# Scores against the context itself: 64-dimension keys replaced by queries widened to 128 dimensions

## The chip, the cores and the metric

The kernel runs on one core of one Trainium2 chip. The metric is the device time in microseconds of one execution, and the number compared is the median of several. A core has five engines that this kernel uses: TensorE (PE, the matrix engine; PEld is its weight load), VectorE (DVE), ScalarE (ACT), GpSimd (POOL), and SyncE (SP), which starts DMAs. They run side by side and meet at semaphores.

## What is computed

Two layers of gated cross-attention, each with a feed-forward block behind it, over 8 batches of 112 queries (width 512) and 375 context rows (width 128). The attention has 16 heads. Of the reference only this matters here (layer 0; layer 1 is the same without the rotation of `q_big`):

```python
q_hk = (hidden_q @ Wq.T).reshape(Bv, Sv, H, K)
q_big = jnp.einsum('bshk,hkq->bshq', q_hk, w_kc_q)
q_big = _apply_rope(q_big, sin_q[None, :, None, :], cos_q[None, :, None, :])
kv_r = _apply_rope(kv_c, sin_k[None], cos_k[None])
q_r = jnp.einsum('bshq,hqr->bhsr', q_big, W_qr)       # 64 dimensions a head
k_r = jnp.einsum('bld,hdr->bhlr', kv_r, W_kr)         # 64 dimensions a head
scores = jnp.einsum('bhsr,bhlr->bhsl', q_r, k_r)
attn = jax.nn.softmax(scores, axis=-1)
ctx_c = jnp.einsum('bhsl,bld->bhsd', attn, kv_r)
```

`scores` is a product of three matrices, q_r times W_kr transposed times kv_r transposed. It can be multiplied from the right first (keys, then scores over 64 rows) or from the left first (queries widened from 64 to 128 dimensions, then scores over 128 rows with the context). Products of this kind are made in float16 with each operand split in a high and a low part, so each takes three matrix products: high by high, high by low, low by high.

## The kernel before

**Stages.** A start (norms, rotation and transposition of the context into `kvT`), attention of layer 0, its output projection mixed with the middle and the first feed-forward block, attention of layer 1, its output projection, the second feed-forward block. In the profile attention 0 lies at about 40 to 420 us and attention 1 at about 560 to 835 us.

**A pair and its slots.** Attention goes over 8 pairs of heads; a pair has 8 slots, one for each batch. Four tables of lists (TENSOR, SCALAR, VECTOR, GPSIMD, lines 70 to 142), one for each engine and layer, say what the engine does in each slot and in which order. All engines execute in order, so a table is the schedule. The items:

- X, scores of this slot's batch (line 759 on PE): six products of 64x128 weights over 375 columns, heads in the upper and the lower 64 rows of the array in turns. On DVE X is the maximum (line 1114). E is the exponential on ACT (line 982), N the reciprocal on DVE (line 1119) and the normalisation on POOL (line 1279).
- T, transposition of the probabilities of two slots before (line 785), split by ACT (line 992) and DVE (line 1182). There is one PSUM area for scores and one for T, so X waits for the exponentials of the slot before, and T for DVE's split of the slot before.
- S, the weighted sum of three slots before (line 800), copied out by ACT (line 998) and DVE (line 1124).
- K, the keys of one batch (line 771): the weights are W_kr of the pair, the moving side is `kvT`. ACT copies them out (line 1008) and POOL splits them into high and low (lines 1268 and 1271).
- A and B (line 813), layer 0: `q_hk` in four half-pairs of 12 products, and `q_big` in 12 blocks of 3 products. DVE takes a B with two products by the rotation tables (line 1137). SP swaps halves of one block by DMA, POOL adds (line 1260).
- C (line 867), layer 0: q_r of a half of the batches. M, W, F with Q, layer 1: the weights are folded first, and F and Q (line 813) make q_r of a half.
- G (line 873) turns W_qr, R (line 877) turns W_kr; U (line 882) prepares the output weights. L and H are the splits of the loaded weights (lines 1193 and 1040), V is work for the feed-forward weights.

**Banks.** Everything but X and T goes round the four PSUM banks 2 to 5 in the order of the PE table. So each group waits until the group four places before it has been taken out by ACT, DVE or both:

```python
bank_of = {g: 2 + i % 4 for i, g in enumerate(groups)}
```

**Last pair.** When there is no next pair to prepare, PE fills the slots with heads of the output projection (line 524; HEADS_AHEAD, lines 147 to 152, says how many).

## Time and profile before

| | us |
|---|---|
| Median of 3 runs | 1024.25 (1022.31 to 1024.72) |
| The profiled execution | 1024.81 |
| Its span, first to last instruction | 1022.8 |
| PE busy / DVE / ACT / POOL | 953.1 / 664.3 / 529.2 / 520.5 |
| Mean granted TensorE clock | 0.987 of full speed |

PE is the busiest engine at 93% of the span; the others are busy for half to two thirds of it. The page gives sums for the whole span, and the stages differ, so the rows below are read from single pairs and slots. A matrix product's bar in the timeline is longer than the time it keeps the array (bars overlap), so what a group costs PE is the distance from its start to the next group's start.

### The profile page before, as it was taken

The page shows a single profiled execution, that of the slowest core. Times are in us where ns is not written, and L with a number is a line of the kernel's source. Part 1 is how long each engine was busy: PE and PEld are TensorE (multiplying, and loading weights), DVE is VectorE, ACT ScalarE, POOL GpSimd, SP SyncE. Part 2 cuts the span into 40 slices and gives each one's busy share as a digit, 9 for nine tenths or more (in the row PEclk, how much of TensorE's full clock was granted, in tenths as well). Part 3 has the DMA queues.
Part 4 walks back from the last instruction along what each step waited for, and adds up shares of the span by engine and source line. Part 5 has one row for each costly group of instructions (what it writes and reads, how often), then busy time and mean ns, then how long its engine had stood idle before and what let it go on. Part 6 is the DMA issues. An engine that isn't in the chain of part 4 may idle for free. (4 is left out here: it accounts for less than half of the span.)

```text
span 1022.8 us, 19581 instructions
## 1 busy us (share of the span) xinstructions
PE 953.1 (93%) x6132; PEld 566.9 (55%) x6141; DVE 664.3 (65%) x1180; ACT 529.2 (52%) x1238; POOL 520.5 (51%) x652
## 2 busy tenths in 40 slices
PE   3679999999999999999889899999999999989998
PEld 1335555555555655644344567777777764445443
DVE  4789777787878787488677757666666653413012
ACT  2255666665766665600377367777777762116300
POOL 4477777776868777405224266665666651200000
PEclk9799999999999999999999999999999999999999
DMA  8214233232314132063020111222012006004001
GB/s 255 66 39 117 61 95 85 69 107 55 115 51 121 49 105 81 15 207 121 0 84 21 61 63 63 72 72 72 14 57 72 1 1 230 7 19 157 1 31 41
DMA packets 30344, 75.56 MB, mean 74 GB/s; under 512 B 4967, under 2 KB 11239, under 8 KB 28126
## 3 DMA queue, kind: packets, MB, share of 16 engines
q1 hardware_dynamic: 24706, 66.31, 20.5%
q10 hardware_dynamic: 5596, 8.70, 3.1%
q8 instruction: 25, 0.41, 0.2%
q14 instruction: 17, 0.14, 0.0%
HBM read 63.98 MB, written 3.68 MB: 66 GB/s over the span
## 5 line engine op out<-in xcount | busy, mean ns | idle before, releaser
L1279 POOL TENSOR_SCALAR scratch<-scratch,rinv 112x375 f32<-112x375 f32 x256 | 154.9, 618 | 138.8 <-DVE rinv L1119 138.8
L982 ACT ACTIVATE scratch<-ps,mxn 112x375 f32<-112x375 f32 x256 | 144.2, 571 | 36.6 <-DVE mxn L1114 35.1
L524 PE MATMUL ps<-arena 128*128 128x512 f16 x672 | 149.3, 379 | 1.2 <-PEq L685 1.2
L1114 DVE TENSOR_REDUCE mxn<-ps 112x2 f32<-112x750 f32 x128 | 119.7, 935 | 41.8 <-PE ps L759 41.3
L1260 POOL TENSOR_TENSOR scratch<-scratch 128x448 f32<-128x448 f32 x64 | 110.7, 1739 | 43.1 <-DVE scratch L1137 27.1
L813 PE MATMUL ps<-xnT,scratch 128*128 128x448 f16 x576 | 124.5, 364 | 6.5 <-DVE scratch L1137 3.3
L800 PE MATMUL ps<-scratch,kvn_hi 125*128 125x224 f16 x768 | 119.9, 260 | 3.3 <-DVE scratch L1159 2.3
L1271 POOL TENSOR_TENSOR scratch<-scratch 128x375 f16<-128x375 f32 x128 | 115.6, 903 | 10.9
L785 PEld LDWEIGHTS ps<-ident,scratch 112*125 112x125 f32 x768 | 101.1, 188 | 26.9 <-issue 19.9
L1182 DVE TENSOR_TENSOR scratch<-ps,scratch 125x672 f16<-125x672 f32 x128 | 108.7, 849 | 5.4 <-ACT scratch L992 5.4
L1137 DVE TENSOR_TENSOR scratch<-ps,ropeq 128x448 f32<-128x448 f32 x192 | 110.0, 616 | 2.1 <-PE ps L813 1.7
L524 PEld LDWEIGHTS ps<-arena 128*128 128x128 f16 x672 | 65.5, 98 | 76.4 <-issue 2.2
L785 PE MATMUL ps<-ident,scratch 112*125 112x112 f32 x768 | 104.8, 272 | 1.1 <-DVE scratch L1182 1.0
L992 ACT ACTIVATE scratch<-ps 125x672 f16<-125x672 f32 x128 | 94.2, 736 | 16.1 <-PE ps L785 15.3
L800 PE MATMUL ps<-scratch,kvn_lo 125*128 125x224 f16 x384 | 99.4, 259 | 0.0
L1159 DVE SCALAR_TENSOR_TENSOR scratch<-ps,scratch 128x448 f16<-128x448 f32 (+2 forms) x88 | 50.0, 569 | 71.8 <-ACT scratch L1026 70.0
L998 ACT ACTIVATE arena<-ps 128x224 f32 (+1 forms) x128 | 45.7, 357 | 95.4 <-PE ps L800 94.7
L1026 ACT ACTIVATE scratch<-ps 128x448 f16<-128x448 f32 (+2 forms) x88 | 43.5, 505 | 89.4 <-PE ps L813 50.5
L813 PEld LDWEIGHTS ps<-xnT,scratch 128*128 128x128 f16 x576 | 57.0, 100 | 59.0 <-issue 9.3
L759 PE MATMUL ps<-scratch 64*128 64x375 f16 x768 | 83.3, 322 | 5.8 <-DVE scratch L1159 4.1
L800 PEld LDWEIGHTS ps<-scratch,kvn_hi 125*128 125x128 f16 x768 | 68.1, 98 | 36.8 <-issue 24.4
L771 PE MATMUL ps<-kvT,scratch 128*128 128x375 f16 x384 | 83.1, 325 | 0.7 <-DVE scratch L1159 0.7
(166 smaller groups left out, 1413.3 us busy)
## 6 DMA issues: line engine op xcount, KB each, us to landing
scratch<-in_wq SPq DMA_DIRECT2D x16, 512.0 KB, 4.5
scratch<-in_wo SPq DMA_DIRECT2D x16, 512.0 KB, 3.7
wabs<-in_w ACTq DMA_DIRECT2D x32, 256.0 KB, 3.0
scratch<-in_w SPq DMA_DIRECT2D x8, 1024.0 KB, 4.9
scratch<-in_W SPq DMA_DIRECT2D x8, 1024.0 KB, 5.9
scratch<-scratch SPq DMA_DIRECT2D x64, 112.0 KB, 2.3
scratch<-in_kcq SPq DMA_DIRECT2D x8, 512.0 KB, 3.4
scratch<-in_qr SPq DMA_DIRECT2D x32, 128.0 KB, 3.3
```

Of the source, the lines that this page charges most:

```text
L524: last = nc.tensor.matmul(ps[:, bank, :], a[:, h, t * P:(t + 1) * P], c[:, h, :], start=(h == 0 and i == 0), stop=(h == H - 1 and i == 2))
L785: last = nc.tensor.transpose(turn_ps[0:LP, c, hh * S:(hh + 1) * S], prob[0:S, s % 2, hh, c * LP:(c + 1) * LP], ident[0:S, 0:S])
L800: last = nc.tensor.matmul(bank(it, ("S", slot))[:, 0:2 * S], kv[0:LP, s, c, :], pr[0:LP, s % 2, cols], start=(c == 0 and i == 0), stop=(c ...
L813: last = nc.tensor.matmul(out, lhs[i](c), rhs[j](c), start=(n == 0), stop=(n == 3 * chunks - 1))
L982: last = nc.scalar.activation(prob[0:S, s % 2, hh, :], scores_ps[0:S, hh, 0:L], ACT.Exp, bias=mxn[0:S, s % 2, hh:hh + 1], accum_out=rsum[0 ...
L992: nc.scalar.activation(probT_hi[0:LP, s % 2, :].rearrange("p (c n) -> p c n", c=LC), turn_ps[0:LP, :, 0:2 * S], ACT.Copy).then_inc(turn_hi ...
L1114: nc.vector.tensor_reduce(mxn[0:S, s % 2, :], scores_ps[0:S, :, 0:L], AX_X, ALU.max, negate=True).then_inc(max_done, 1)
L1137: last = nc.vector.tensor_tensor(dst.rearrange("p (b n) -> p b n", b=B // 2), src, ropeq[:, t:t + 1, :].to_broadcast([P, B // 2, S]), ALU. ...
L1182: nc.vector.tensor_tensor(probT_lo[0:LP, s % 2, :].rearrange("p (c n) -> p c n", c=LC), turn_ps[0:LP, :, 0:2 * S], probT_hi[0:LP, s % 2, : ...
L1260: nc.gpsimd.tensor_tensor(roped[:, u % 2, rows], roped[:, u % 2, rows], turned[:, rows], ALU.add)\
L1271: nc.gpsimd.tensor_tensor(kr_lo[:, b % 2, 0:L], kr[:, b % 2, 0:L], kr_hi[:, b % 2, 0:L], ALU.subtract).then_inc(k_ready, 1)
L1279: last = nc.gpsimd.tensor_scalar(prob[0:S, s % 2, hh, :], prob[0:S, s % 2, hh, :], rinv[0:S, s % 2, hh:hh + 1], P_SCALE, ALU.mult, ALU.mult)
```

## The change

Keys, their copy on ACT and their split on POOL are gone (K), and so is R. Instead the half's 64-row queries (C in layer 0, Q in layer 1) are split into `q64_hi` and `q64_lo`, and a new group P, two banks wide, multiplies them by W_kr: six products of 64x128 weights over 448 columns, heads in the upper and the lower 64 rows of the array in turns. ACT and DVE split each bank of it into `qw_hi` and `qw_lo`, 128 dimensions wide. W_kr is no longer turned by PE; it is split where it was loaded (a third weight split, H 2 on ACT and L 2 on DVE). Scores are six products of 128x128 weights over 375 columns, whose moving side is `kvT`. The weights of a batch differ from product to product.

```diff
-        kr, a = view(scratch, a, [2, LPAD], F32)
-        kr_hi, a = view(scratch, a, [2, LPAD], F16)
-        kr_lo, a = view(scratch, a, [2, LPAD], F16)
-        qr_hi, a = view(scratch, a, [B, P], F16)
-        qr_lo, a = view(scratch, a, [B, P], F16)
+        q64_hi, a = view(scratch, a, [HALF], F16)
+        q64_lo, a = view(scratch, a, [HALF], F16)
+        qw_hi, a = view(scratch, a, [2 * B, P], F16)
+        qw_lo, a = view(scratch, a, [2 * B, P], F16)
...
-                        for i, (a, b) in enumerate(((qr_hi, kr_hi), (qr_hi, kr_lo), (qr_lo, kr_hi))):
-                            for hh in range(2):
-                                rows = slice(hh * R, (hh + 1) * R)
-                                last = nc.tensor.matmul(scores_ps[:, hh, 0:L], a[rows, s, :],
-                                                        b[rows, s % 2, 0:L],
+                        for hh in range(2):
+                            for i, (a, j) in enumerate(((qw_hi, 0), (qw_hi, 1), (qw_lo, 0))):
+                                last = nc.tensor.matmul(scores_ps[:, hh, 0:L], a[:, hh, s, :],
+                                                        kvT[:, j, s * L:(s + 1) * L],
                                                         start=(i == 0), stop=(i == 2))
...
-                        for i, (v, j) in enumerate(((wkr_hi, 0), (wkr_hi, 1), (wkr_lo, 0))):
-                            last = nc.tensor.matmul(bank(p, g)[:, 0:L], v,
-                                                    kvT[:, j, b * L:(b + 1) * L],
-                                                    start=(i == 0), stop=(i == 2))
-                        last.then_inc(k_done, 1)
...
+                            pe.wait_ge(split_lo, nth_half(q, "qr"))
+                            for i, (a, b) in enumerate(((wkr_hi, q64_hi), (wkr_hi, q64_lo),
+                                                        (wkr_lo, q64_hi))):
+                                for h in range(2):
+                                    rows = slice(h * R, (h + 1) * R)
+                                    last = nc.tensor.matmul(bank(p, ("P", n, h))[:, 0:HALF], a[rows],
+                                                            b[rows], start=(i == 0), stop=(i == 2))
...
-                        nc.gpsimd.tensor_copy(kr_hi[:, b % 2, 0:L], kr[:, b % 2, 0:L])\
-                            .then_inc(k_high, 1)
-                        pool.wait_ge(k_high, nth(q, B, b))
-                        nc.gpsimd.tensor_tensor(kr_lo[:, b % 2, 0:L], kr[:, b % 2, 0:L],
-                                                kr_hi[:, b % 2, 0:L],
-                                                ALU.subtract).then_inc(k_ready, 1)
```

The tables are written anew. In layer 0 each preparation group of a next pair comes one slot earlier against X, and the P groups stand in slots 3 and 7, in front of B. In layer 1 they stand in slots 1 and 6. One row of PE's table and one of DVE's, layer 0:

```diff
-    [TURN, SCORES, *ropes(0, 2, 0), ("S", 4), ("K", 6), ("A", 1)],
+    [TURN, SCORES, *wide(1), *ropes(0, 2, 0), ("S", 3), ("A", 1)],
...
-    [SCORES, *ropes(0, 2), TURN, *ropes(0, 0), NORM, ("S", 4), ("A", 1)],
+    [SCORES, TURN, *wide(1), *ropes(0, 2, 0), NORM, ("S", 3), ("A", 1)],
```

**What moves on PE, slot with two B and an A.** Layer 0, the loop over pairs, from the scores on; before, slot 0:

```order
L759 MATMUL ps<-scratch 128x375 x6
L851 REGISTER_ALU
L852 ISA
L813 MATMUL ps<-scratch 128x448 x3
L658 REGISTER_ALU
L813 MATMUL ps<-scratch 128x448 x3
L656 REGISTER_ALU
L800 MATMUL ps<-scratch,kvn_hi 128x224 x2
```

In the changed kernel, slot 3 (L764 is the scores, L862 is P, L806 is B, L793 is S, L670 prepares a wait for a bank):

```order
L764 MATMUL ps<-kvT,scratch 128x375 x6
L833 REGISTER_ALU
L857 REGISTER_ALU
L862 MATMUL ps<-scratch 128x448 x6
L670 ISA
L866 REGISTER_ALU
L806 MATMUL ps<-scratch 128x448 x6
L670 REGISTER_ALU
L793 MATMUL ps<-scratch,kvn_hi 128x224 x2
```

P has come between the scores and the two B. P takes two banks, so S is now the fourth bank after P's first, and waits for DVE to take that one out.

**What moves on DVE, the same slots.** Before (L1114 maximum, L1137 rotation of a B, L1182 split of T), slot 4, whose items are those of slot 0:

```order
L1114 TENSOR_REDUCE mxn<-ps 112x2
L1163 ISA
L1176 REGISTER_ALU
L1137 TENSOR_TENSOR scratch<-ps,ropeq 128x448 x2
L1182 TENSOR_TENSOR scratch<-ps,scratch 125x672
L1163 REGISTER_ALU
L1137 TENSOR_TENSOR scratch<-ps,ropeq 128x448 x2
```

In the changed kernel, slot 3, behind the maximum (L1184 split of T, L1160 of 128x4x112 the low part of a P bank, L1140 rotation):

```order
L1184 TENSOR_TENSOR scratch<-ps,scratch 125x672
L1152 REGISTER_ALU
L1160 SCALAR_TENSOR_TENSOR scratch<-ps,scratch 128x4x112
L1152 REGISTER_ALU
L1160 SCALAR_TENSOR_TENSOR scratch<-ps,scratch 128x4x112
L1164 ISA
L1178 REGISTER_ALU
L1140 TENSOR_TENSOR scratch<-ps,ropeq 128x448 x2
L1164 REGISTER_ALU
L1140 TENSOR_TENSOR scratch<-ps,ropeq 128x448 x2
```

The two low parts of P stand behind the maximum and T's split, and ahead of both rotations.

**What moves on PE where a slot with two B ends.** Before, the end of slot 2 and the start of slot 3 of layer 0 (L771 the keys, L882 U, L785 T):

```order
L800 MATMUL ps<-scratch,kvn_lo 128x224
L662 REGISTER_ALU
L771 MATMUL ps<-kvT,scratch 128x375 x3
L662 REGISTER_ALU
L880 ISA
L882 MATMUL ps<-scratch 128x512
L785 MATMUL ps<-ident,scratch 125x112 x6
L759 MATMUL ps<-scratch 128x375 x6
```

In the changed kernel, the end of slot 1 and the start of slot 2 (L892 is U, L778 is T):

```order
L793 MATMUL ps<-scratch,kvn_lo 128x224
L670 REGISTER_ALU
L890 ISA
L892 MATMUL ps<-scratch 128x512
L778 MATMUL ps<-ident,scratch 125x112 x6
L761 REGISTER_ALU
L764 MATMUL ps<-kvT,scratch 128x375 x6
```

The keys have gone from between S and U, so T follows its slot's S by U alone.

## Rows read from the trace of the kernel before

**Rows 1.** Busy time by engine, one pair of each layer (us, times).

```profile
core 0: us, PE busy (x) PEld busy (x) DVE busy (x) ACT busy (x) POOL busy (x), PEclk, DMA share, GB/s
213.00:259.50 46.50, 45.42 (x311) 27.38 (x309) 37.34 (x69) 29.79 (x76) 34.39 (x41) 1.00 0.30 85
689.80:721.70 31.90, 31.55 (x254) 23.28 (x253) 21.60 (x41) 22.94 (x63) 20.10 (x33) 1.00 0.18 58
```

**Rows 2.** Timeline of PE, layer 0: start us, us, operation; around G and R.

```profile
281.09 0.49 PE L873 MATMUL ps<-ident,scratch 128*128 128x128 f32 x3
282.14 0.33 PE L877 MATMUL ps<-ident,scratch 128*128 128x128 f32 x1 [0.56 <-DVE scratch L1137]
282.50 0.74 PE L813 MATMUL ps<-scratch 128*128 128x448 f16 x3
...
327.59 0.49 PE L873 MATMUL ps<-ident,scratch 128*128 128x128 f32 x3
```

**Rows 3.** Timeline of PE, layer 1, a slot from T to G.

```profile
655.50 0.60 PE L785 MATMUL ps<-ident,scratch 112*125 112x112 f32 x4
656.03 0.65 PE L759 MATMUL ps<-scratch 64*128 64x375 f16 x6
656.62 0.36 PE L800 MATMUL ps<-scratch,kvn_hi 125*128 125x224 f16 x2
...
657.49 0.65 PE L771 MATMUL ps<-kvT,scratch 128*128 128x375 f16 x3
657.97 0.49 PE L873 MATMUL ps<-ident,scratch 128*128 128x128 f32 x3
```

**Rows 4.** Timeline of PE, layer 0: T before slot 0, then slot 2.

```profile
248.70 0.81 PE L785 MATMUL ps<-ident,scratch 112*125 112x112 f32 x6
249.77 0.49 PE L759 MATMUL ps<-scratch 64*128 64x375 f16 x4 [0.26 <-DVE scratch L1159]
...
258.93 0.81 PE L785 MATMUL ps<-ident,scratch 112*125 112x112 f32 x6
259.67 0.65 PE L759 MATMUL ps<-scratch 64*128 64x375 f16 x6
260.25 1.31 PE L813 MATMUL ps<-scratch 128*128 128x448 f16 x6
261.39 0.36 PE L800 MATMUL ps<-scratch,kvn_hi 125*128 125x224 f16 x2
...
262.26 0.64 PE L771 MATMUL ps<-kvT,scratch 128*128 128x375 f16 x3
263.04 1.10 PE L882 MATMUL ps<-scratch 128*128 128x512 f32 x2
263.97 0.81 PE L785 MATMUL ps<-ident,scratch 112*125 112x112 f32 x6
```

**Rows 5.** Timeline of DVE in the same slot 2.

```profile
260.71 0.93 DVE L1114 TENSOR_REDUCE mxn<-ps 112x2 f32<-112x750 f32 x1
261.64 1.16 DVE L1137 TENSOR_TENSOR scratch<-ps,ropeq 128x448 f32<-128x448 f32 x2
262.72 0.85 DVE L1182 TENSOR_TENSOR scratch<-ps,scratch 125x672 f16<-125x672 f32 x1
```

**Rows 6.** Timeline of all engines, last pair of layer 1, one slot of the scores' loop.

```profile
825.56 0.65 PE L759 MATMUL ps<-scratch 64*128 64x375 f16 x6
...
826.26 0.94 DVE L1114 TENSOR_REDUCE mxn<-ps 112x2 f32<-112x750 f32 x1 [0.73 <-PE ps L759]
...
827.11 0.85 DVE L1182 TENSOR_TENSOR scratch<-ps,scratch 125x672 f16<-125x672 f32 x1
827.22 0.36 ACT L998 ACTIVATE arena<-ps 128x224 f16<-128x224 f32 x1 [0.82 <-PE ps L800]
...
828.48 0.21 ACT L982 ACTIVATION_READ_ACCUMULATOR scratch<-ps,mxn 112x1 f32 x1
...
828.92 0.49 PE L759 MATMUL ps<-scratch 64*128 64x375 f16 x4
```

**Rows 7.** Groups by line and shape: ACT's high part and DVE's low part.

```profile
L1159 DVE SCALAR_TENSOR_TENSOR scratch<-ps,scratch 128x448 f16<-128x448 f32 x64 | 39.9, 624 | 60.9 <-ACT scratch L1026 59.0
L1026 ACT ACTIVATE scratch<-ps 128x448 f16<-128x448 f32 x64 | 35.1, 548 | 77.5 <-PE ps L813 50.5 <-PE ps L867 27.0
```

More of the change, by code:

```diff
@@ L530, in attention @@
             groups = [g for slot in TENSOR[layer] for g in slot if g[0] not in MARKS]
-            order = [g for g in groups if g[0] not in ("S", "K", "F")]
+            order = [g for g in groups if g[0] not in ("S", "F")]
             groups = [g for g in groups if g[0] != "Q"]
@@ L628, in pair_of @@
             def pair_of(p, g):
-                return p if g in this or (g[0] == "K" and g[1] >= 2) else p + 1
+                return p if g in this else p + 1
+            own_banks = {(-1, ("W", 0)): 2} if layer == 1 else {}
+            for it, slots in ((PAIRS - 1, range(2 if layer == 0 else 0, B)), (PAIRS, range(3))):
+                for s in slots:
+                    for g in TENSOR[layer][s]:
+                        if g in groups and runs(it, g):
+                            own_banks[it, g] = 2 + len(own_banks) % 3
             def bank_at(p, g):
-                return last_banks.get((p, g), bank_of[g]) if isinstance(p, int) else bank_of[g]
+                return own_banks.get((p, g), bank_of[g]) if isinstance(p, int) else bank_of[g]
             def bank(p, g):
@@ L823, in group @@
                             return
-                        if kind == "K":
-                            keys(p, g)
-                            return
                         q, hh = pair_of(p, g), n % 2
                         out = bank(p, g)
-                        if kind != "Q":
+                        if kind == "P":
+                            latest = (0, at["C" if layer == 0 else "Q", n])
+                            for x in wide(n):
+                                last, back = bank_before(p, x)
+                                if last is not None and last[0] == "S":
+                                    wait_bank(pe, p, x)
+                                elif last is not None:
+                                    last = ("Q", last[1]) if last[0] == "F" else last
+                                    latest = max(latest, (-back, at[last]))
+                            if g[2] == 0:
+                                return
+                            last = order[latest[1]]
+                            pe.wait_ge(group_out, nth_group(pair_of(p + latest[0], last), last))
+                        elif kind != "Q":
                             wait_bank(pe, p, g)
@@ L1231, in iteration @@
                                     norm_low(dve, n0, t, t % 2)
-                            if layer == 0 and first(p) and s == 6:
+                            if layer == 0 and first(p) and s == 5:
                                 kv_rope(dve, nc.vector, 4)
@@ L1685, in vector @@
                 norm_apply(dve, m, 5, x_sb)
-                ahead(("R", 0))
                 finish(6)
```

296 lines of the change are left out of this document (131 added, 165 removed), and 2 rows, old and new, of the table HEADS_AHEAD.

## The prediction, made before the changed kernel was run

> **What bounds the kernel now.** I read the busy time of a pair of each layer first. In layer 0 PE is busy for 45.42 of 46.50 us, in layer 1 for 31.55 of 31.90, while no other engine passes 37.34 and 22.94 [rows 1]. The granted clock is 1.00 in both, the 2.4 GHz level. So attention is bound by PE, and where PE stands still it is for a moment, behind another engine's late result. The question is then twofold: how much array time the change adds or takes, and which short waits go and come. Pairs repeat: G starts at 281.09 and again at 327.59, 46.50 us later [rows 2]. So I work in us for a pair, from group start to group start.
>
> **PE's array time.** Keys take 657.97 - 657.49 = 0.48 us for three products over 375 columns, 0.16 each [rows 3]. Scores take 0.59 (656.62 - 656.03) for six: they run as three pairs, an upper and a lower half of the array at once. Three times 0.16 would be 0.48, so 0.10 more is paid when they are left. Another 0.10 is paid when they are entered: four transpositions start at 655.50, and with 0.11 between them the fourth starts at 655.83, but the scores start 0.20 after that. At both edges the next weights are not loaded under the running product. Over all 128 rows, six scores cost 6 x 0.16 = 0.96, with neither edge: T falls from 0.74 (259.67 - 258.93 in [rows 4]) to 0.64, and scores go from 0.58 to 0.96. Net +0.28 for each slot, against -0.48 for the keys: -0.20 x 8 = -1.6. P is new: three pairs over 448 columns. Two B, six products of that length, take 261.39 - 260.25 = 1.14 [rows 4], so 0.19 each; P costs 3 x 0.19 and both edges, 0.77, twice a pair: +1.54. If its halves did not overlap it would be 2.3 for both, the upper bound. R goes, -0.11 (a quarter of what G and R need). Sum: -0.2 us for a pair, with bounds -0.4 and +0.6. On array time alone the change is worth 3 us of 1024.
>
> The Trainium skill, TensorEngine Tiling (Array Packing), sections Theoretical Speedup and Key Properties, gives up to twice the throughput for a contraction of at most 64 rows, and says that a change of tiling mode drains the engine. By its factor of two alone, unpacking would double 0.58 to 1.17 a slot, 4.7 us for a pair instead of my 2.2, and the whole change would cost PE 2.3 a pair. The rows show both edges of the packed form, 0.10 each, which is why I use 0.28; the keys' own rows are full-array products over these columns.
>
> **Other engines.** POOL loses 16 instructions a pair (cast and subtraction of the keys). It is idle for a quarter of the pair [rows 1] and nothing on PE waits for it, so I cost this at nothing; at best it makes SBUF work on DVE a little faster. ACT loses eight copies and gets four high parts of 0.55 [rows 7] and one small weight split. DVE loses R's split and gets four low parts of 0.62, about +2 us on 37.3, and a small weight split. DVE is the second engine of layer 0, and it is full in some slots. SP only gets its weight load of W_qr with W_kr behind one more swap, early enough: it has more than a slot to land.
>
> **Waits that go, layer 0.** G and R take 282.50 - 281.09 = 1.41 for 0.44 of work, because R's bank is still with DVE [rows 2]: -0.97. U starts 0.78 behind the keys' start instead of 0.48, again a bank [rows 4]: -0.30. X behind C waits for C's split: T takes 1.07 instead of 0.74 [rows 4]; the other place of this kind is smaller. P now stands between and starts after T and X, 1.60 behind C's end, about when the split is ready: -0.5 for both. Together -1.8 for a pair.
>
> **Waits that come, layer 0.** First, S behind P (slots 3 and 7). Take 0 as the start of the scores. S could start at 0.96 + 0.77 + 1.14 = 2.87. Its bank is P's first. DVE begins the maximum 0.70 after the scores' start now [rows 6], and 0.46 later when the last product starts at 0.80 instead of 0.33: 1.16. The maximum takes 0.85 (827.11 - 826.26), T's split 0.8, P's low part 0.62: done at 3.4, S at 3.5. Wait 0.6, twice: +1.2. Second, T behind a slot with two B (slots 2 and 6). T needs DVE's split of the slot before. From the maximum of the slot before that, DVE has no pause: 0.85, 0.8, a B of 1.07 (262.72 - 261.64 in [rows 5]), 0.36 of small steps, a B of 1.07, then the maximum, a B and the split, 0.85 + 1.07 + 0.85. That is 6.9 from 1.16 on, so T can start at 8.2 with 0.15 for the weights. PE arrives at 3.60 (X, B, S, B, T) plus 3.83 (X, two B, S, U) = 7.4: wait 0.75, and 0.85 where G's copy lies in between. Before, the same chain began at 0.70 and PE had the keys twice: 7.7 against 7.7, just covered, as 263.57 (262.72 + 0.85) against a T at 263.97 shows. So +1.6. Together +2.8, and layer 0 makes -0.2 - 1.8 + 2.8 = +0.8 for a pair. I take +0.7, since DVE's splits of weights may be shorter with POOL emptier; over 8 pairs +5.6.
>
> **Waits, layer 1.** PE idles 0.35 in the pair [rows 1], and the timeline's bars hide about as much again; these are banks of Q and R and go: -0.6. New: U in slot 1 gets the bank of S of the same slot, which DVE frees at 1.16 + 0.85 + 0.8 + 0.38 = 3.2, while PE is there at 0.96 + 0.87 + 0.77 + 0.33 = 2.9; with the weights of U +0.45. In slot 6 the two low parts and U's stand ahead of slot 7's maximum on DVE, which comes 0.6 late and so does the T behind it: +0.5. Then the loop of the scores: ACT takes S's copy at 827.22, 1.66 after the scores' start, and ends the exponentials at 828.69, 3.13 after it [rows 6]. With scores longer by 0.37 this is 3.50, and the next scores start 0.15 later, at 3.65. A slot with only F or Q would need 0.64 + 0.96 + 0.87 + 1.13 = 3.60, so +0.05 in four slots. Sum -0.2 - 0.6 + 0.45 + 0.5 + 0.2 = +0.35, for 7 pairs +2.5. In the last pair the slots take 828.92 - 825.56 = 3.36 [rows 6], of which PE needs 3.35; they become 3.65 in six slots: +1.7. The head of layer 1 loses one R and one K, -0.6. The last pair of layer 0 has the same bound, but PE's keys went there too; its four slots and the start, where DVE is full, I leave at 0 with 3 either way.
>
> **Sum.** 5.6 + 2.5 + 1.7 - 0.6 = 9.2, less 1 to 2 for what hand schedules double (a wait in one slot gives DVE time that the next no longer lacks): +7.5. The profiled execution took 1024.81, 2.0 more than its span and 0.6 more than the median of 1024.25. I put the change on the median: **1032 us**.
>
> **Rivals.** (a) The new waits cost as much as those that go. This needs S behind P or T behind two B to be covered, for instance because DVE reaches P's low part half a microsecond earlier. Each pair in both layers then makes -0.2 to 0.2: 1021 to 1027. (b) Faster. The waits that go are seen in rows, the new ones are my schedule. If none comes, layer 0 makes -0.2 - 1.8 = -2.0 and layer 1 -0.8: 8 x -2.8 = -22 at most; with the scores' loop still holding the last pair (+1.7), 1004 to 1015. For it: PE has slack of only 0.1 in many places before and no wait shows there. Against it: DVE's chain is made of the same instructions as before, it starts 0.46 later, and PE comes 0.3 earlier. (c) Much slower. P's halves don't overlap on the array (+0.75 a pair, +12) or the scores' loop binds most slots of layer 1, because ACT must also make P's high parts ahead of the next T split. That decides once ACT's split of T is later than the maximum's end: then each slot of layer 1 takes 3.9 to 4.1 instead of 3.65, about 1 us a pair more. With one of them 1040 to 1048. (d) That the change does not do what it says: the order shows P, full-height scores and no keys, so I leave this at nothing.
>
> **Chances.** Forecast, 1028 to 1038: 0.50. Rival (a): 0.20. Rival (b): 0.18. Rival (c): 0.12. The range for 8 in 10 takes in (a), the upper half of (b) and the start of (c): 1012 to 1042. A measurement of this kernel tells about 0.3%, 3 us, from no change. Slower by more than that: the forecast and (c), and the upper edge of (a), 0.64. Within: 0.16. Faster: (b) and a little of (a), 0.20.
>
> **What would show it.** In the profile after: scores six in 0.96 and T in 0.64; P in 0.77; in layer 0 the S behind P starts 0.6 late with DVE named, and T of slots 2 and 6 starts late with DVE's split of T named; a layer-0 pair of about 47.2 and a layer-1 pair of about 32.2; slots of 3.65 in the last pair of layer 1. I am wrong if G's and U's waits went and no other came, if a pair of layer 0 is under 46.2, or if the scores cost other than 0.16 a product.

## The result: 3.3% slower, and the profile of the changed kernel

The changed kernel takes 1058.33 us (median of four executions, 1054.52 to 1059.18), the kernel before 1023.33 beside it on the same chip. The ratio is 1.0334, with a 95% interval of 1.0317 to 1.0351. The direction was predicted, the size was not: 1032 was the forecast, 1042 the upper end of the range, and 34 us came where 8 were expected.

The profiled execution of the changed kernel took 1054.52, with a span of 1052.7. First the two rows that answer to [rows 1], a pair of each layer (a pair repeats every 49.28 and every 32.60 us now):

```profile
core 0: us, PE busy (x) PEld busy (x) DVE busy (x) ACT busy (x) POOL busy (x), PEclk, DMA share, GB/s
203.77:253.05 49.28, 45.58 (x297) 27.64 (x296) 41.99 (x73) 27.68 (x72) 23.04 (x24) 1.00 0.29 80
680.00:712.60 32.60, 32.01 (x242) 23.76 (x240) 23.67 (x44) 21.81 (x59) 9.33 (x16) 1.00 0.18 56
```

In layer 0 PE's busy time is what it was, 45.58 against 45.42, and the pair is 2.78 longer: 3.70 of it PE is idle now, against 1.08. POOL has lost 11 us of work, as the diff says. But DVE, the engine that was to get 2 us more, got 4.65 more (41.99 against 37.34). So some instruction on DVE became slower. The groups of PE's waits in the whole execution (what it waited for, us, times, longest) name it:

```profile
engine line waited for: us in total, times, longest us
PE ps L806 <- DVE scratch L1198: 16.0, 8, 3.5
PE ps L778 <- DVE scratch L1184: 15.5, 30, 0.9
...
PE ps L793 <- DVE scratch L1160: 6.8, 14, 1.4
```

Before, the first of them was 6.3 us in three waits. L806 is A, the projection of a pair's queries; L1198 is DVE's split of the weights, here of wq. The second is T behind DVE's split of T, 0.85 each, and the third S behind P. These two were predicted (of the 30 waits behind DVE's split of T about half, 9.6 us, are in layer 0; 10 are in layer 1). The first was not.

Where the 30 us between the two profiled spans (1022.8 and 1052.7) were lost, by the starts of the scores:

| stretch | before | after | more |
|---|---|---|---|
| up to the first scores | 58.6 | 60.5 | 1.9 |
| layer 0, first to last scores | 362.7 | 376.1 | 13.4 |
| to the first scores of layer 1 | 168.1 | 175.3 | 7.2 |
| layer 1, first to last scores | 246.2 | 253.8 | 7.6 |
| to the end | 187.2 | 187.1 | 0 |

And a pair slot by slot, from one start of scores to the next, for slots 0 to 7:

| | 0 | 1 | 2 | 3 | 4 | 5 | 6 | 7 | pair |
|---|---|---|---|---|---|---|---|---|---|
| layer 0, after | 3.72 | 5.37 | **9.02** | 7.24 | 3.93 | 5.41 | 7.34 | 7.24 | 49.28 |
| layer 1, before | 3.81 | 3.87 | 4.01 | 4.46 | 3.81 | 3.92 | 3.93 | 4.06 | 31.87 |
| layer 1, after | 3.72 | 4.99 | 3.82 | 4.27 | 3.72 | 3.73 | 4.19 | 4.16 | 32.60 |

Slots 2 and 6 of layer 0 hold the same kinds of products, and one takes 1.68 longer than the other. Here is slot 2 in the timelines of PE, DVE and POOL (start us, us, engine, line, operation; in brackets the idle time before and what ended it):

```profile
217.24 0.88 PE L778 MATMUL ps<-ident,scratch 112*125 112x112 f32 x6 [0.67 <-DVE scratch L1184]
217.95 1.12 PE L764 MATMUL ps<-kvT,scratch 128*128 128x375 f16 x6
...
219.68 0.26 PE L793 MATMUL ps<-scratch,kvn_lo 125*128 125x224 f16 x1
221.44 2.44 PE L806 MATMUL ps<-xnT,scratch 128*128 128x448 f16 x12 [1.51 <-DVE scratch L1198]
```

```profile
217.00 1.15 DVE L1140 TENSOR_TENSOR scratch<-ps,ropeq 128x448 f32<-128x448 f32 x2
218.07 0.38 DVE L1127 SCALAR_TENSOR_TENSOR arena<-ps,arena 128x224 f32 x1
218.37 0.15 DVE L1122 RECIPROCAL rinv<-rsum 112x2 f32<-112x2 f32 x1
218.44 2.95 DVE L1198 SCALAR_TENSOR_TENSOR scratch<-scratch 128x1024 f16<-128x1024 f32 x1
```

```profile
217.08 3.22 POOL L1265 TENSOR_TENSOR scratch<-scratch 128x448 f32<-128x448 f32 x2 [1.00 <-DMA scratch<-scratch]
220.28 2.13 POOL L1273 TENSOR_SCALAR scratch<-scratch,rinv 112x375 f32<-112x375 f32 x2
```

A stands still for 1.5 us, because DVE's split of wq takes 2.95 us. POOL's line is two rotary additions; the second (896 elements) begins at 218.23 and lasts 2.08, to 220.31. DVE had begun its split 0.21 us after that, and ends it 1.08 after the addition's end. In the kernel before, the same two instructions met in the other order (timelines of DVE, then of POOL, of before; they stand at the end of the lists of the slot of [rows 5], and A behind them belongs to the next slot on PE):

```profile
264.91 1.38 DVE L1193 SCALAR_TENSOR_TENSOR scratch<-scratch 128x1024 f16<-128x1024 f32 x1
...
262.63 0.50 POOL L1268 CAST scratch<-scratch 128x375 f16<-128x375 f32 x1
263.21 0.90 POOL L1271 TENSOR_TENSOR scratch<-scratch 128x375 f16<-128x375 f32 x1
264.07 4.16 POOL L1260 TENSOR_TENSOR scratch<-scratch 128x448 f32<-128x448 f32 x2
```

There POOL still had to cast and subtract a block of keys, so its additions began at 264.07 and 265.16, and the second came 0.26 **after** DVE's split had started. DVE took 1.38, and it was POOL's second addition that took 3.06 instead of 2.08. Nobody waited for it. Of the 4.65 us that DVE got more in a pair this split is 1.57 (2.95 against 1.38). The other 3.1 are the four low parts of P, less R's split, and the new third split of weights in slot 5: 128x128, 0.29 where nothing is in its way, 1.62 here behind another of POOL's additions (DVE at 195.35, POOL from 194.73 to 196.82). Nobody waits for that one.

So the theory to be tested: the work on keys that the change took from POOL had been what kept the addition behind the split. The rival is that the longer scores or the new order tables made the split late in some other way.

The Trainium skill states such a rule under SBUF — State Buffer, section Who interferes with whom: VectorE and GpSimd share one pair of ports, an instruction of VectorE with two SBUF inputs contends with one of GpSimd that reads SBUF, and whichever issues first keeps the pair for its whole length. The split has two SBUF inputs (the raw weights and their high part). The numbers of this meeting agree: the split takes 1.20 where no addition is in its way (e1, e2), and where it waits it ends 1.08 behind the addition; at 218.44 the rest of the addition (1.87) plus 1.08 is 2.95, which is what the row shows. One meeting in e1, below, does not go by the order of the recorded starts. The prediction did not weigh this page; it should have.

### The profile page after: what moved, and what is told of

The parts are those of the page before. It is cut to its first block and busy times, and to the rows that moved or that the text cites. A ratio compares the mean times of both kernels' runs of the same rounds, so it can differ in the third digit from the quotient of the medians.

```text
span 1052.7 us, 18579 instructions
## 1 busy us (share of the span) xinstructions
PE 960.3 (91%) x5924; PEld 574.5 (55%) x5933; DVE 714.1 (68%) x1244; ACT 503.7 (48%) x1174; POOL 340.7 (32%) x396
## 5 line engine op out<-in xcount | busy, mean ns | idle before, releaser
L764 PE MATMUL ps<-kvT,scratch 128*128 128x375 f16 x768 | 143.8, 323 | 3.0 <-DVE scratch L1160 1.5
L806 PE MATMUL ps<-xnT,scratch 128*128 128x448 f16 x576 | 123.9, 362 | 14.4 <-DVE scratch L1198 12.8
L778 PEld LDWEIGHTS ps<-ident,scratch 112*125 112x125 f32 x768 | 96.8, 188 | 62.4 <-issue 48.9
L1265 POOL TENSOR_TENSOR scratch<-scratch 128x448 f32<-128x448 f32 x64 | 104.6, 1641 | 74.1 <-DVE scratch L1140 39.0
L793 PE MATMUL ps<-scratch,kvn_hi 125*128 125x224 f16 x768 | 119.3, 259 | 6.8 <-DVE scratch L1160 6.8
L778 PE MATMUL ps<-ident,scratch 112*125 112x112 f32 x768 | 109.6, 279 | 15.7 <-DVE scratch L1184 15.5
L1160 DVE SCALAR_TENSOR_TENSOR scratch<-ps,scratch 128x448 f16<-128x448 f32 (+1 forms) x136 | 82.2, 625 | 56.3 <-ACT scratch L1026 55.4
L1026 ACT ACTIVATE scratch<-ps 128x448 f16<-128x448 f32 (+1 forms) x136 | 71.0, 549 | 95.2 <-PE ps L806 47.6
L1184 DVE TENSOR_TENSOR scratch<-ps,scratch 125x672 f16<-125x672 f32 x128 | 108.5, 848 | 5.0 <-ACT scratch L1002 5.0
L1140 DVE TENSOR_TENSOR scratch<-ps,ropeq 128x448 f32<-128x448 f32 x192 | 108.6, 615 | 1.0 <-issue 0.4
L793 PE MATMUL ps<-scratch,kvn_lo 125*128 125x224 f16 x384 | 99.3, 259 | 0.0
L764 PEld LDWEIGHTS ps<-kvT,scratch 128*128 128x128 f16 x768 | 75.6, 99 | 37.7 <-DVE arena L1155 3.0
L806 PEld LDWEIGHTS ps<-xnT,scratch 128*128 128x128 f16 x576 | 56.6, 100 | 62.7 <-issue 11.6
L793 PEld LDWEIGHTS ps<-scratch,kvn_hi 125*128 125x128 f16 x768 | 73.3, 98 | 28.8 <-DVE scratch L1160 10.2
L806 PE MATMUL ps<-scratch 128*128 128x448 f16 x288 | 66.5, 360 | 3.6 <-DVE scratch L1198 3.2
```

What stands on the lines that cost most here:

```text
L764: last = nc.tensor.matmul(scores_ps[:, hh, 0:L], a[:, hh, s, :], kvT[:, j, s * L:(s + 1) * L], start=(i == 0), stop=(i == 2))
L778: last = nc.tensor.transpose(turn_ps[0:LP, c, hh * S:(hh + 1) * S], prob[0:S, s % 2, hh, c * LP:(c + 1) * LP], ident[0:S, 0:S])
L793: last = nc.tensor.matmul(bank(it, ("S", slot))[:, 0:2 * S], kv[0:LP, s, c, :], pr[0:LP, s % 2, cols], start=(c == 0 and i == 0), stop=(c ...
L806: last = nc.tensor.matmul(out, lhs[i](c), rhs[j](c), start=(n == 0), stop=(n == 3 * chunks - 1))
L1140: last = nc.vector.tensor_tensor(dst.rearrange("p (b n) -> p b n", b=B // 2), src, ropeq[:, t:t + 1, :].to_broadcast([P, B // 2, S]), ALU. ...
L1184: nc.vector.tensor_tensor(probT_lo[0:LP, s % 2, :].rearrange("p (c n) -> p c n", c=LC), turn_ps[0:LP, :, 0:2 * S], probT_hi[0:LP, s % 2, : ...
```

## Experiments on the collision

**e5.** The kernel before, with POOL's work on the keys nearly gone in layer 0. It leaves out most of the keys' high and low parts there, so its scores are not the reference's. The edit (two memsets at the start, which zero those parts, are not shown):

```diff
-  nc.gpsimd.tensor_copy(kr_hi[:, b % 2, 0:L], kr[:, b % 2, 0:L])
+  n = 2 if layer == 0 else L
+  nc.gpsimd.tensor_copy(kr_hi[:, b % 2, 0:n], kr[:, b % 2, 0:n])
...
-  nc.gpsimd.tensor_tensor(kr_lo[:, b % 2, 0:L], ...
+  nc.gpsimd.tensor_tensor(kr_lo[:, b % 2, 0:n], ...
```

> This is the kernel BEFORE, with one thing taken from POOL: in layer 0 it casts and subtracts 2 of the 375 columns of each block of keys, so most of the keys' high and low parts stay zero there (that part of the computation is left out). PE, ACT and DVE keep every instruction. Theory: POOL's work on the keys was what kept its addition of the rotary halves behind DVE's split of wq. Without it the addition starts 0.2 to 0.5 us before the split, keeps the port, and the split takes 2.7 to 3.0 us instead of 1.38; A behind it waits about 1.5 us in slot 3 of each of seven pairs. A kernel with LESS work becomes SLOWER: 1031 to 1036 us against 1023.5, and a layer-0 pair grows from 46.5 to 47.7 to 48.0. Rival: POOL's load as such costs DVE time and nothing hangs on the order, so less work is 0 to 4 us faster (1019 to 1024). Second rival: the collision needs the new order tables as well: then the same time within 0.3%.

Measured: 1031.07 us, ratio 1.0064 [1.0045, 1.0082]; a pair of layer 0 went from 46.51 to 48.17. Nothing else of the change is in this kernel, and with less work it is 6.8 us slower than the 1024.29 beside it. The median is at the lower edge of what was expected, because the start with the first pair became 2 us shorter and the stretch before layer 1 another 1; the pair's 1.66 is a little more than the 1.2 to 1.5 that were expected. The slot with A grew from 7.79 to 9.45. Timelines of DVE, POOL and PE:

```profile
268.05 3.04 DVE L1193 SCALAR_TENSOR_TENSOR scratch<-scratch 128x1024 f16<-128x1024 f32 x1
...
266.84 3.17 POOL L1260 TENSOR_TENSOR scratch<-scratch 128x448 f32<-128x448 f32 x2 [0.60 <-DMA scratch<-scratch]
...
271.15 0.74 PE L813 MATMUL ps<-xnT,scratch 128*128 128x448 f16 x3 [1.68 <-DVE scratch L1193]
```

The additions begin at 266.84 and 267.93, the second 0.12 before the split; it ends at 270.01, and 1.08 later the split is done. Both rivals fall: with less load on POOL the kernel is slower and not faster, and the new tables are not needed for it.

**e2.** The other way round: the changed kernel, with work put back on POOL. After each normalisation in layer 0, POOL casts 320 columns of a table and subtracts them, for nothing:

```diff
+  nc.gpsimd.tensor_copy(idle, src)
+  nc.gpsimd.tensor_tensor(idle, src, idle, ALU.subtract)
```

> The changed kernel with useless work added to GpSimd in layer 0: after each normalisation a cast and a subtraction over 320 columns of the rotation table into an unused buffer, about the work that the keys' split was. Theory (the order in which the two engines reach the shared reads decides): more work on GpSimd makes its additions start later, VectorE's split of wq goes first again and takes 1.4, and the kernel gets faster by 5 to 12 us in spite of the added work. Rival (GpSimd's work is off the path and its amount makes nothing): no change within 3 us, or slower where the added work itself collides.

Measured: 1045.75 us, ratio 1.0219 [1.0201, 1.0238], so 12 us less than the changed kernel without that work. Slot 2 fell from 9.02 to 7.34, the value of slot 6, in the five pairs where it had been 9.02, all other slots of these pairs stayed, and the pair is 47.59. That is 8.4 of the 12; the rest of the difference between the medians is no slot of layer 0 (see **Sum** below). Timelines of POOL and DVE:

```profile
214.86 0.45 POOL L1292 CAST scratch<-ropeq 128x320 f16<-128x320 f32 x1
215.39 0.79 POOL L1295 TENSOR_TENSOR scratch<-ropeq,scratch 128x320 f16<-128x320 f32 x1
216.14 4.27 POOL L1267 TENSOR_TENSOR scratch<-scratch 128x448 f32<-128x448 f32 x2
...
217.27 1.20 DVE L1200 SCALAR_TENSOR_TENSOR scratch<-scratch 128x1024 f16<-128x1024 f32 x1
```

**e1.** The same without extra work, by order: POOL normalises before its second addition, `[*ropes(3, 2, 1), NORM]` becomes `[*ropes(3, 2), NORM, *ropes(3, 1)]` in slot 1, and likewise in slot 5.

> The changed kernel, with GpSimd's second rotary addition of slots 1 and 5 of layer 0 put behind the normalisation of the slot; nothing else moves. Theory (GpSimd and VectorE shut each other out while both read SBUF; since the keys' split is gone, GpSimd starts its 2.1 us addition 0.2 us ahead of VectorE's split of wq, which then takes 2.95 us instead of 1.38): the split takes 1.1 to 1.4 again, the products behind it start about 1.6 us earlier, a pair of layer 0 goes from 49.28 to about 47.7 and the kernel gets 10 to 12 us faster. Rival (the wait comes from VectorE's own greater load, the collision only fills it): the split gets short but a pair stays within 0.3 of 49.28.

Measured: 1050.29 us, ratio 1.0279 [1.0234, 1.0323]; slot 2 is 8.05. The split takes 1.20 and A no longer waits. But the addition now ends so late that C waits for it, which the expectation had missed (POOL, then PE):

```profile
220.63 2.08 POOL L1265 TENSOR_TENSOR scratch<-scratch 128x896 f32<-128x896 f32 x1
...
222.84 0.97 PE L881 MATMUL ps<-scratch 128*64 128x448 f32 x4 [0.64 <-POOL scratch L1265]
```

That is the point of the two orders: the addition may not come early, for DVE's sake, nor late, for C's.

The same order in slot 5 shows a limit of the reading by recorded starts (DVE, then POOL):

```profile
243.65 3.06 DVE L1198 SCALAR_TENSOR_TENSOR scratch<-scratch 128x128 f16<-128x128 f32 x1
...
243.35 1.17 POOL L1273 TENSOR_SCALAR scratch<-scratch,rinv 112x375 f32<-112x375 f32 x2 [0.26 <-DVE rinv L1122]
244.48 2.08 POOL L1265 TENSOR_TENSOR scratch<-scratch 128x896 f32<-128x896 f32 x1
```

The small split, 0.29 elsewhere, is recorded 0.83 before the addition, while POOL normalises, and still ends 0.15 behind the addition, in every pair of this run. Two normalisations and the addition went ahead of it in a row. So being recorded first is not enough; what decided here stays open. PE did not wait for it.

**e3.** The split of T ahead of the two B on DVE, in slots 1 and 5: `[SCORES, *ropes(3, 0), TURN, *ropes(3, 1), ...` becomes `[SCORES, TURN, *ropes(3, 0, 1), ...`. It was made for the second wait in the list, T of slots 2 and 6.

> The changed kernel with VectorE's order in slots 1 and 5 of layer 0 changed from scores, rotation, split of the turned probabilities, rotation to scores, split, rotation, rotation. Theory (the transposition of slots 2 and 6 starts 0.85 late each because the split of the slot before stands behind a rotation): both waits go, U's start-to-next falls from 1.70 and 1.74 to 0.86, a pair gets 1.0 to 1.7 shorter and the kernel 8 to 13 us faster, unless the split of wq, which stands later in slot 1, still holds the products of slot 2: then only slot 6 gains, 0.85 a pair, 6 to 7 us. Rival (VectorE's total load in these slots is the bound): less than 3 us.

Measured: 1038.45 us, ratio 1.0144 [1.0126, 1.0162]: 19 us less than the changed kernel, more than expected. Slots 1 and 5 fell by 0.6 each, which is the wait it was made for, and slot 2 from 9.02 to 7.65 as well. In the pair whose scores of slot 2 begin near 213 the profile shows by how little. The views of POOL's addition line and of DVE's split, in a window of 2.5 us (instructions, duration min/median/max in ns, first and last start):

```profile
L1265 POOL TENSOR_TENSOR scratch<-scratch x2: 1145/2158/3172, 212.5 to 213.6; 128x448 f32<-128x448 f32 x1, 128x896 f32<-128x896 f32 x1
...
L1198 DVE SCALAR_TENSOR_TENSOR scratch<-scratch x1: 1199/1199/1199, 213.7 to 213.7; 128x1024 f16<-128x1024 f32 x1
```

The second addition is recorded first, by less than 0.1 us, and still it is the one that waits (3.17 instead of 2.08) while the split takes 1.20. The start that a trace records is thus not exactly the moment at which one of them has the port; as close as this the rows don't tell who wins (and e1's slot 5 shows a case at 0.83 us). The 1.4 us in slot 2 were not what this edit was made for: by the rows the split came first by luck, with starts a few hundredths of a microsecond apart.

**e4.** One B between P and S in slots 3 and 7 of layer 0, on PE: `*wide(1), *ropes(0, 2, 0), ("S", 3)` becomes `*wide(1), *ropes(0, 2), ("S", 3), *ropes(0, 0)`.

> The changed kernel with PE's order in slots 3 and 7 of layer 0 changed from P, block 2, block 0, S to P, block 2, S, block 0, so that S gets another bank and block 0 the first bank of P. Theory (S starts 0.59 late, since its bank is P's first, which VectorE frees 3.4 us after the scores' start): block 0 comes to that bank 0.3 later than S did, so a wait of 0.2 to 0.3 stays and 0.3 to 0.4 goes, twice a pair: the kernel gets 4 to 6 us faster. Rival (the wait moves to the next group on PE, since VectorE is behind anyway): within 2 us.

Measured: 1054.29 us, ratio 1.0288 [1.0256, 1.0321]. Slots 3 and 7 fell from 7.24 to 6.94 each, 0.6 a pair. That is 0.3 of each wait of S behind P (0.58, twice a pair), as expected: by this order half of it can be undone.

## Experiments on layer 1

**e6.** The exponentials ahead of the copy of S on ACT, in all slots of layer 1: `[TURN, ("S", 0), EXPS, ...]` becomes `[TURN, EXPS, ("S", 0), ...]`.

> The changed kernel, with one order swapped in all eight slots of layer 1 on ACT: the exponentials ahead of the copy of S. Theory: in the slots with nothing but F or Q, and in the last pair, the slot of 3.72 is the loop scores, maximum, exponentials, scores, and the copy of S (0.5 to 0.6 us) stands in it. With the exponentials first the loop is about 3.2 and PE's own 3.60 takes over where F or Q stands; in the last pair, where PE needs 2.5 to 3.4, slots fall from 3.72 to about 3.5, since S's bank comes later. Sum: 8 x 0.1 x 4 + 6 x 0.2 = 3 to 5 us faster than the changed kernel, 1050 to 1056 us. Rival: PE's own work, not that loop, sets 3.72, and the later copy of S holds DVE and the next S: no gain or 1 to 4 us slower, slots of 3.72 to 3.9.

Measured: 1064.23 us, ratio 1.0393 [1.0376, 1.0410], 6 us slower. No slot got shorter, the 3.72 of the last pair stayed 3.72, and slot 1 grew from 4.99 to 6.00, because U waits there for the bank that S leaves:

```profile
654.87 1.10 PE L892 MATMUL ps<-scratch 128*128 128x512 f32 x2 [1.28 <-DVE arena L1127]
```

So ACT's loop does not set the slot. The timelines of PE and DVE in the last pair of the changed kernel show the one that does:

```profile
850.75 1.12 PE L764 MATMUL ps<-kvT,scratch 128*128 128x375 f16 x6
853.76 0.88 PE L778 MATMUL ps<-ident,scratch 112*125 112x112 f32 x6 [0.38 <-DVE scratch L1184]
854.48 1.12 PE L764 MATMUL ps<-kvT,scratch 128*128 128x375 f16 x6
...
851.91 0.94 DVE L1117 TENSOR_REDUCE mxn<-ps 112x2 f32<-112x750 f32 x1 [1.20 <-PE ps L764]
852.77 0.85 DVE L1184 TENSOR_TENSOR scratch<-ps,scratch 125x672 f16<-125x672 f32 x1
```

The next T needs its bank, which DVE frees with the split of the T before; that split stands behind the maximum, and the maximum behind the scores: 1.16 + 0.86 + 0.85 + 0.14 to T, + 0.72 to the next scores.

**e9.** The split of T ahead of the maximum on DVE in layer 1: `[SCORES, TURN, ...]` becomes `[TURN, SCORES, ...]` in all eight slots.

> The changed kernel, with one order swapped in all slots of layer 1 on DVE: the split of T ahead of the maximum instead of behind it. Theory, formed after the exponentials were moved in vain: the slot of 3.72 is a loop of PE and DVE and not one of ACT. T must wait until DVE has split the T before; that split stands behind the maximum, and the maximum behind the scores: 1.16 from the scores' start to the maximum, 0.86 for it, 0.85 for the split, 0.14 to T's start and 0.71 to the next scores: 3.72. With the split first, PE's own work sets the slot: 3.35 to 3.40 in six slots of the last pair, 3.60 where F or Q stands. Sum: 6 x 0.35 + 7 x (3 x 0.12) + slot 7 (4.16 to between 3.7 and 4.16): 4 to 8 us faster than the changed kernel, 1047 to 1054 us. Rival: the later maximum makes the exponentials late and the loop scores, maximum, exponentials takes over: slots of 3.7 to 4.3, no gain or slower.

Measured: 1071.32 us, ratio 1.0457 [1.0440, 1.0475]. The rival was right in kind; slots 1, 2 and 7 are longer than its 3.7 to 4.3 (4.88, 4.71 and 5.01). T no longer waits, but the slots of the last pair are 3.63 and now the scores wait for ACT's exponentials; other slots grew (slot 2 from 3.82 to 4.71, slot 7 from 4.16 to 5.01).

```profile
879.91 0.96 PE L764 MATMUL ps<-kvT,scratch 128*128 128x375 f16 x5 [0.35 <-ACT scratch L992]
```

The loop that the prediction had named, scores to exponentials and 3.65, can be read from the changed kernel itself (ACT, in the slot that starts at 850.75):

```profile
854.03 0.21 ACT L992 ACTIVATION_READ_ACCUMULATOR scratch<-ps,mxn 112x1 f32 x1
```

The exponentials end 3.49 after the scores' start (3.50 was forecast); with the 0.15 to the next scores this loop would give 3.64. It lies right behind the one of 3.72. The 3.63 of e9 is a neighbour of it, not the same: T's split stands ahead of the maximum there.

**e11.** The kernel before, with the swap of e9.

> The kernel BEFORE with the same swap on DVE in layer 1 (the split of T ahead of the maximum). Before, PE's own work sets the last pair's slots (3.35) and most of the others, so by the loop theory nothing is to be won there: within 0.3% of 1024, with slots of 3.35 in the last pair as they are and a pair of 31.4 to 32.0. If it gains more than 3 us, the loop held the kernel before too.

Measured: 1048.04 us, ratio 1.0228 [1.0208, 1.0247]. Neither expectation held: the last pair's slots went from 3.35 to 3.98. The order maximum first is worth 24 us to the kernel before, and nothing was held by the other loop there. The trace shows where the 3.98 come from (PE, then DVE):

```profile
843.15 0.65 PE L759 MATMUL ps<-scratch 64*128 64x375 f16 x6 [0.59 <-ACT scratch L982]
...
844.03 0.86 DVE L1182 TENSOR_TENSOR scratch<-ps,scratch 125x672 f16<-125x672 f32 x1 [0.83 <-ACT scratch L992]
844.80 0.93 DVE L1114 TENSOR_REDUCE mxn<-ps 112x2 f32<-112x750 f32 x1
```

T's split waits for ACT's high part of T, so the maximum begins 1.65 after the scores and not 0.70; the exponentials follow it, and the next scores, at 847.13, follow them.

**e7.** The low part of U(1) on DVE moved from slot 6 to slot 7 of layer 1, behind the split of T.

> The changed kernel, with the low part of U(1) on DVE in layer 1 moved from the end of slot 6 to slot 7, behind the split of T. Theory: slot 7 takes 4.16 where PE needs 3.60 because three low parts (two of P, one of U) stand ahead of the next maximum on DVE. One of them (0.69) moved: slot 7 falls by 0.4 to 0.55 in each of eight pairs, 3 to 4.5 us in all, a layer-1 pair from 32.60 to 32.1. Rival: ACT's two copies for P make the split of T late, not DVE's: slot 7 stays at 4.1 to 4.2 and the time within 0.1%.

Measured: 1053.73 us, ratio 1.0292 [1.0275, 1.0309]; slot 7 fell from 4.16 to 3.73 and the pair to 32.16, all as expected. Three low parts ahead of a maximum did cost 0.43, where the prediction gave 0.5 for slot 7.

## All orders together

**e8** takes e3, e4, e6 and e7, puts the split of wq ahead of the small normalisation step, and makes the split of W_kr for layer 1's first pair (the expectations call it W_qr, with which it is loaded) ahead of Q's parts instead of after the last normalisation. It was written before e6 was known.

> The changed kernel with all orders that this study found better, and no work left out: DVE splits T ahead of the two B of slots 1 and 5 of layer 0; one B stands between P's successor S and P in slots 3 and 7; the split of wq ahead of the small normalisation step; exponentials first on ACT in layer 1; the low part of U(1) in slot 7; the split of W_qr for the first pair of layer 1 before Q's parts instead of behind the last normalisation. Expected from the earlier runs: a layer-0 pair of 45.8 to 46.1 (46.5 before), a layer-1 pair of 31.6 to 32.0 (31.9 before), the head of layer 1 about 1 us shorter: 1022 to 1030 us, so the change as such is worth nothing or little once its waits are gone. If PE's array time of the change is what costs (rival), the pair of layer 0 cannot go under 46.5 and the time stays above 1030.

Measured: 1038.12 us, ratio 1.0128 [1.0107, 1.0149]. The 1022 to 1030 were missed by 8 us. Layer 0 came as expected, a pair of 46.02; layer 1 has e6's 6.00 in slot 1 and a pair of 33.17. **e10** is e8 with e9's swap instead of e6's and the split of wq also ahead of the low part of S.

> All orders of the run before it but the exponentials' (that one cost 1.02 in slot 1 of layer 1), with the split of T ahead of the maximum in layer 1 and the split of wq also ahead of the low part of S. No work is left out against the changed kernel. If the last theory holds: a layer-0 pair of 45.7 to 46.0, a layer-1 pair of 31.0 to 31.9, slots of 3.35 to 3.4 in the last pair: 1018 to 1027 us. If the split before the maximum only moves the wait: a layer-1 pair of 32.2, slots of 3.7 and 1028 to 1033 us.

Measured: 1048.68 us, ratio 1.0228 [1.0202, 1.0254]: layer 0 at 45.98, layer 1 at 34.3, so both of its expectations failed too. **e12** leaves both swaps of layer 1 out and keeps the rest.

> The changed kernel with only the orders that held in the runs before: in layer 0 the split of T ahead of the two B, the split of wq ahead of the low part of S, one B between S and its predecessor P; in layer 1 the low part of U(1) later; at the head of layer 1 the split of W_qr earlier. No work is left out. Expected from the pieces as measured: up to the last scores of layer 0, 4 us ahead of the kernel before (417 against 421); the stretch from there to layer 1's first scores 4 to 5.5 us longer than before (the last four slots of layer 0, P's stage at the head); layer 1 0.3 x 7 + 2.3 longer. Sum: +4 to +6: 1027 to 1031 us, still slower than the kernel before by 0.4 to 0.7%. Rival: the pieces disturb each other as the exponentials' order did, and it stays at 1035 or more.

Measured: 1030.54 us, ratio 1.0060 [1.0046, 1.0074]. By order alone, with every product of the changed kernel, 28 of its 34 us are gone, and a pair of layer 0 is shorter than in the kernel before (45.98 against 46.51). One pair of each layer and the first pair of layer 1:

```profile
200.00:245.98 45.98, 45.47 (x297) 27.73 (x295) 40.32 (x73) 27.47 (x71) 23.04 (x24) 1.00 0.31 86
...
650.00:682.16 32.16, 31.90 (x243) 23.76 (x239) 23.57 (x45) 21.70 (x59) 9.33 (x16) 1.00 0.19 63
...
590.20:623.50 33.30, 31.73 (x213) 21.90 (x213) 21.10 (x39) 19.65 (x53) 8.14 (x14) 0.95 0.29 95
```

PE is busy for 45.47 of 45.98. What remains, by spans (1030.0 against 1022.8): up to layer 0's last scores it is 5.1 ahead, the stretch between the layers 5.9 longer, layer 1 is 6.3 longer (six pairs by 0.29, the last by 2.2, the first by 2.4). No version tried beats the kernel before.

## Why the prediction was right and wrong

**PE's array time: right.** Scores take 0.96 for six, T 0.64, P 0.77 with its entry, as worked out. PE's busy time for a pair of layer 0 rose by 0.16 in the changed kernel and by 0.05 in e12, where -0.2 was forecast and +0.6 was the upper bound. A factor of two between packed and full array is not what this kernel shows: scores went from 0.58 to 0.96, not to 1.17.

**Waits that go: right.** G and R's 0.97 is gone with R: G stands alone with 0.33. U follows S without a wait in layer 0.

**Waits that come in layer 0: right, with small errors.** T of slots 2 and 6 starts 0.85 and 0.88 late (0.75 and 0.85 forecast), S behind P 0.58 (0.6 forecast):

```profile
242.84 0.88 PE L778 MATMUL ps<-ident,scratch 112*125 112x112 f32 x6 [0.70 <-DVE scratch L1184]
...
230.42 0.36 PE L793 MATMUL ps<-scratch,kvn_hi 125*128 125x224 f16 x2 [0.41 <-DVE scratch L1160]
```

With the collision removed (e2) the pair is 47.59, where the forecast was 47.2: all of layer 0 but one term was right to 0.4 a pair.

**The step that failed: "POOL loses 16 instructions a pair ... I cost this at nothing; at best it makes SBUF work on DVE a little faster".** The term was taken as a gain of 0.1 a pair. It cost 1.68 in slot 2 of five pairs and nothing that shows in the others (1.66 a pair in e5, where it stands alone). What misled was the question asked: who waits for POOL, and is it busy. Nobody does, and it isn't. But POOL's work was also the delay that decided which of two instructions came first, and the rows that show it (264.07 for POOL, 264.91 for DVE) are not among those that the prediction rests on. The term was given no upper side, although the trace before shows the meeting: POOL's addition takes 3.06 there beside others of 2.08, and DVE's split 1.38 beside 1.20. How long the split gets when it comes second, 2.95, that trace does not show.

This term alone does not explain why the range failed: without the collision e2 still takes 1045.75, above the upper end of 1042. The second step that failed is the next one, and it is nearly as large.

**The second step that failed, the head of layer 1 ("loses one R and one K, -0.6"): +4.5 measured.** From Q's products to the first scores it was 5.14 before and is 9.65 (timeline of PE):

```profile
602.21 2.43 PE L806 MATMUL ps<-xnT,scratch 128*128 128x448 f16 x12
604.89 0.66 PE L352 MATMUL ps<-ident,scratch 128*128 128x128 f32 x4 [0.24 <-DVE scratch L342]
607.25 1.20 PE L862 MATMUL ps<-scratch 64*128 64x448 f16 x6 [1.71 <-DVE scratch L1198]
608.37 2.08 PE L892 MATMUL ps<-scratch 128*128 128x512 f32 x2
611.86 1.13 PE L764 MATMUL ps<-kvT,scratch 128*128 128x375 f16 x6 [1.41 <-DVE arena L1155]
```

I counted the R and the K that go, and not that P is one more stage of a chain with nothing beside it: Q, its split, P, U, U's two parts on ACT and DVE, and the scores. P waits for the split of W_kr, which stood behind the last normalisation on ACT and DVE. U (L892) stands behind P now; it is its low part (L1155) that the first scores wait for, since PE starts the first pair only when all preparation groups are taken out, in the kernel before too (there 0.76, with U at 586.99, beside Q's splits). After PE's wait the granted clock fell (columns as in [rows 1]):

```profile
606.00:607.20 1.20, 0.00 (x0) 0.00 (x0) 0.89 (x2) 0.38 (x2) 0.00 (x0) 1.00 0.00 0
608.40:610.50 2.10, 2.05 (x4) 0.47 (x2) 1.16 (x2) 0.99 (x3) 0.00 (x0) 0.50 0.77 199
```

From 608.40 to 610.50 it is 0.50, the 1.2 GHz level (0.82 over the whole stretch). P takes 1.20 and U 2.08 here, against 0.74 and 1.12 at full clock in e12, 1.4 together. In e12, with the split earlier, the same stretch is 7.22. The rest of the 7.2 between the layers lies in layer 0's last slots and the projection; it was left open within 3, and I did not take it apart.

**Layer 1: right in kind, half in size.** A pair grew by 0.73 where +0.35 was forecast, the last pair by 2.25 where 1.7 was. The waits of U in slot 1 and ahead of slot 7 came as told (e7). The slots of 3.65 are 3.72, in six slots of the last pair and in three of each other, for a loop of PE and DVE that the prediction did not list. The deduction of 1 to 2 us for what a hand schedule counts double had nothing to stand on.

**Sum.** Forecast +7.5; measured +30 between the profiled spans. Of the 22.5 between them the collision is 8.4 in the traces (5 x 1.68; by the medians of e2 and the changed kernel it is 12, but these differ in more than the collision), the stretch between the layers 7.8 (7.2 against -0.6; 5.1 of it at the head), layer 1 3.4 (7.6 against 4.2), the start 1.9; the last 1.0 is the deduction just named, 1.7, less 0.6 by which the rest of layer 0 stayed under its forecast. The median of the changed kernel is another 4 us above its profiled execution. In the profiles of e2, e3, e4, e6 and e7 the clock falls once more in the first pair of layer 1 (e7's took 34.51 at a granted clock of 0.91, the changed kernel's 31.91 at 1.00, e1's 31.90 at 1.00), and the changed kernel's other executions have a mean clock of 0.982, as e7's profile (0.983) and not as its own profile (0.988); that this is the 4 us is likely and not shown. It bears on e2 as well: its other executions have 0.985 to 0.986, which fits the part of the 12 us that no slot of layer 0 holds.

```profile
610.88:645.39 34.51, 32.90 (x213) 22.34 (x214) 21.02 (x39) 19.62 (x53) 8.11 (x14) 0.91 0.26 84
```

## What to carry to other kernels

Work that is taken from an engine that nobody waits for is not free to take: look at what that engine does next, when it will now start, and which instruction of another engine it will meet there. In the trace before, an instruction whose duration varies between repetitions of one shape (here 2.08 and 3.06, 1.20 and 1.38) marked such a pair. And where a hand-written order gets a longer stage, list every loop through a bank (scores, maximum, split, next T), not only the one that was last before: here the one that set the slot, 3.72, and the one that the prediction had, 3.64, lie 0.08 us apart.

## What the runs showed of the hardware

In these runs a split on DVE with two SBUF inputs (128x1024) and an addition on POOL over SBUF (128x896) did not run side by side: one waited for the other's whole instruction. The split takes 1.20 us where nothing is in its way. Where it comes second it takes 1.08 and what is left of POOL's addition at its start: 2.95 with 1.87 left, 3.04 with 1.96 left (e5), 1.38 in the kernel before with 0.30 left (of the addition of 448 elements, 264.07 + 1.14), 1.45 with 0.37 left (e12). When the split comes first, the addition takes 3.06 instead of 2.08. Between the kernel before and e5 the second addition's start moved by 0.38 us against the split's (from 0.26 behind to 0.12 ahead), and that moved 1.66 us onto DVE. The recorded starts mostly tell who waits, and not always: at 0.03 us the one recorded first waited (e3), and in e1 a split recorded 0.83 us ahead of the addition, during a normalisation on POOL, waited for all three instructions.
